# Attention block with layer norm and a gated network on one core: output matmuls over ten steps, max rows by two DMAs in f16, 40 units' lead, and first-pass matmuls in pairs behind the scores

## The reference

```python
qk = (x @ Wqk_w.T + Wqk_b).reshape(b, n, H, E, 2)     # q = qk[..., 0], k = qk[..., 1]
v = (x @ Wv_w.T + Wv_b).reshape(b, n, H, E)
scores = einsum('bhqd,bhkd->bhqk', q, k)
attn = softmax(scores, axis=-1) / sqrt(64)
out = einsum('bhsl,bhlv->bhsv', attn, v) -> (b, n, 64)
x = layernorm(x + out @ Wo_w.T + Wo_b)
# gated network: int4 weights with a float scale for each group of 128 inputs, 1792 inner values
y = einsum('bsi,hi->bsh', silu(x @ Wg.T) * (x @ Wu.T), Wd)
x = layernorm(x + y)
```

## Time and profile before

| | before |
|---|---|
| median of the runs | 572.08 us (571.86, 572.08, 576.48) |
| profiled execution | 576.28 us |
| its span, first to last instruction | 574.5 us |
| mean granted clock of PE | 0.968 |
| PE busy | 531.3 us (92%) |
| DVE busy | 422.3 us (74%) |
| ACT busy | 406.5 us (71%) |
| POOL busy | 234.2 us (41%) |
| chain of waits by engine | PE 72%, DVE 19%, ACT 3%, issue 2%, DMA 2% |
| largest lines of the chain | L842, L854, L871 (network) 50%; L971 (first-pass reduction) 14%; L793 (av) 5%; L726 (first pass) 5%; L760 (output matmul) 3% |
| L971 reductions | 256 of 682 ns mean |
| L557 exponentials | 128 of 1115 ns mean |
| L842, L854, L871 | 448 matmuls each, 379 ns mean (pipelined) |
| L1092, L1112 DVE scaling | 755 and 750 ns mean |

### The profile page before, as it was taken

The page is one execution under the profiler, slowest core; times in us unless marked ns, Lnnn a source line. Parts: engine busy times, 40 slices in busy tenths (PEclk is TensorE's granted clock), DMA queues, the critical chain, the costliest instruction groups (busy, mean ns, idle before and its releaser), DMA issues.

```text
span 574.5 us, 7484 instructions
## 1 busy us (share of the span) xinstructions
PE 531.3 (92%) x2640; PEld 198.7 (35%) x2640; DVE 422.3 (74%) x725; ACT 406.5 (71%) x579; POOL 234.2 (41%) x267
## 2 busy tenths in 40 slices
PE   9897888989889989989999999999999999999992
PEld 3222212222122212214444445444454444544441
DVE  3589796978898799244877678766688667787666
ACT  1430675757677768997788877878878887787881
POOL 8020740002291255263546332673334733338442
PEclk9899597979999999999999999999999999999998
DMA  5593175002231003021004000010000010000101
GB/s 174 160 192 66 40 138 181 1 2 57 91 37 39 3 0 76 2 47 28 1 1 56 18 2 0 2 63 12 0 2 1 0 74 0 2 1 1 73 2 73
DMA packets 29237, 24.59 MB, mean 43 GB/s; under 512 B 19632, under 2 KB 21552, under 8 KB 29200
## 3 DMA queue, kind: packets, MB, share of 16 engines
q1 hardware_dynamic: 25328, 17.56, 11.4%
q0 software_dynamic: 3872, 6.56, 5.9%
HBM read 20.08 MB, written 4.19 MB: 42 GB/s over the span
## 4 chain that ended last, share of the span: by engine, by line
PE 72%; DVE 19%; ACT 3%; issue 2%; DMA 2%; SPq 1%; POOL 0%; POOLq 0%; ACTq 0%; DVEq 0%
PE ps L842 17%; PE ps L854 17%; PE ps L871 16%; DVE mxh L971 14%; PE ps L793 5%; PE ps L726 5%; PE ps L760 3%; PE ps L666 3%; PE ps L778 2%; PE ps L712 2%; ACT pbuf L557 1%; DMA stack<-mp 1%; SPq L335 1%; PE ps L880 1%; DVE st L1010 1%
## 5 line engine op out<-in xcount | busy, mean ns | idle before, releaser
L971 DVE TENSOR_REDUCE mxh<-ps 128x1 f32<-128x512 f32 x256 | 162.1, 682 | 28.4 <-PE ps L726 26.9
L1092 DVE TENSOR_SCALAR ps<-ps,ratio 128x512 f32<-128x512 f32 x168 | 121.8, 755 | 80.9 <-PE ps L854 80.5
L557 ACT ACTIVATE pbuf<-ps,gamma 128x1024 f32<-128x1024 f32 x128 | 135.2, 1115 | 49.7 <-PE ps L778 49.3
L612 ACT ACTIVATE ps<-ps,ratio 128x512 f32<-128x512 f32 x168 | 106.0, 657 | 41.7 <-PE ps L842 41.7
L871 PE MATMUL ps<-stack,wd 128*128 128x512 f16 x448 | 129.5, 379 | 0.6 <-POOL stack L484 0.6
L842 PE MATMUL ps<-arena,wg 128*128 128x512 f16 x448 | 115.3, 379 | 0.1
L854 PE MATMUL ps<-arena,wu 128*128 128x512 f16 x448 | 115.3, 379 | 0.0
L633 ACT ACTIVATE ps<-ps,ratio 128x512 f32<-128x512 f32 x156 | 102.7, 664 | 16.4 <-PE ps L871 16.4
L726 PE MATMUL ps<-stack 64*128 64x512 f16 x256 | 89.6, 407 | 13.6 <-DVE mxh L971 9.3
L482 POOL CAST stack<-pbuf 128x512 f16<-128x512 f32 x56 | 34.1, 609 | 141.3 <-DVE pbuf L1099 141.3
L793 PE MATMUL ps<-pbuf,arena 128*32 128x512 f32 x512 | 71.2, 629 | 0.6 <-ACT pbuf L557 0.6
(11 more groups left out here) (100 smaller groups left out, 330.5 us busy)
## 6 DMA issues: line engine op xcount, KB each, us to landing
arena<-xT SPq DMA_DIRECT2D x16, 256.0 KB, 5.6
x<-x SPq DMA_DIRECT2D x2, 2048.0 KB, 10.1
out<-x SPq DMA_DIRECT2D x3, 1024.0 KB, 4.2
wg<-gq POOLq DMA_DIRECT2D x4, 448.0 KB, 10.3
wu<-uq POOLq DMA_DIRECT2D x4, 448.0 KB, 12.7
wd<-dq POOLq DMA_DIRECT2D x2, 896.0 KB, 10.7
out<-x SPq DMA_DIRECT2D x4, 256.0 KB, 2.4
stack<-mp SPq DMA_DIRECT2D x48, 2.0 KB
```

The costliest lines, as they stand in the source:

```text
L557: nc.scalar.activation(pbuf[:, pi % 4, :].rearrange("p (a n) -> p a n", a=2), ps[:, 2 * (pi % 2):2 * (pi % 2) + 2, :], ACT.Exp, scale=gamm ...
L612: nc.scalar.activation(gbank[t % 2], gbank[t % 2], ACT.Copy, scale=gr[:, t % G, c:c + 1])\
L971: nc.vector.tensor_reduce(mxh[:, f % 2, qh, half:half + 1], ring_bank("first", n, 0), AX.X, ALU.max)\
L1092: nc.vector.tensor_scalar(ubank[t % 2], ubank[t % 2], ur[:, t % G, c:c + 1], None, ALU.mult)\
```

## The change

Eight things change together.

1. PE's order in a step becomes scores, a, b, scores, c, d, (others), av; `ring_at` puts the other uses behind the four units.
2. The output matmuls of a block lie at steps 4, 7, 10, 13 of the next block (ten steps from first to last) instead of 4, 6, 7, 8. The statistics move from steps 9, 10 to 14, 15. DVE's application of block 2's norm (and POOL's splitting) moves from step 12 of the last block into the network's periods 5 to 8, block 3's from periods 7 to 10 into 11 to 14.
3. The maxima are split into three f16 parts before the transpose, on 128x16, inside `combine`; one f16 transpose of 48 columns and one DVE copy (`max_out`) follow. M comes one step later (n+2 divisible by 8) and waits for `s_mrow`.
4. `max_rows` issues two DMAs, each of 24 partitions x 128 f16 into three rows, instead of six.
5. `AHEAD` is 40 instead of 46; the first M stands behind 34 units instead of 37.
6. `place_rows` issues batch 1's rows from two queues: twelve DMAs by POOL, twelve by SP between the scale loads and the second group's max rows.
7. Before step 0 two `put` pieces follow each two units (one piece behind two units once 15 are left), and two puts instead of three precede the first unit.
8. v of batch 1 is transposed into bank 6 and placed by DVE in step 0; `scores(0, 0)` waits only for its own banks, `av(0)` for v.

```diff
-AHEAD = FG + 14
+AHEAD = FG + 8
@@ ring_at
-            f, r = divmod(n + 3, KT)
+            f, r = divmod(n + 2, KT)
...
-            return first[0:2] + other + first[2:4]
-        WO_AT = (4, 6, 7, 8)
+            return first + other
+        WO_AT = (4, 7, 10, 13)
         before = [("first", n, 0) for n in range(AHEAD)]
-        before.insert(FG + 5, ("M", 0, 0))
+        before.insert(FG + 2, ("M", 0, 0))
@@ new, called by SP with jj = 1 and by POOL with jj = 0
+        def place_rows(engine, jj):
+            for kind in range(2):
+                for part in range(2):
+                    for slot in range(4)[half_slots(kind, part)]:
+                        r, at = ROWS * jj + E * slot, kind * HD + jj * HD // 2
+                        src = (high, low)[part][at:at + HD // 2, :]
+                        if kind:
+                            engine.dma_start(ks[1][r:r + E, :, :], src).then_inc(s_stk1[jj], 16)
+                            continue
+                        for k in range(N // TB):
+                            engine.dma_start(qs[1][r:r + E, k, :, :], src[:, k * TB:(k + 1) * TB])\
+                                .then_inc(s_stk1[jj], 16)
@@ max_rows
-                for i in range(3):
-                    for jj in range(2):
-                        r = ROWS * jj + MROW + i
-                        sp.dma_start(qs[b][r:r + 1, k, 2 * g:2 * g + 2, :],
-                                     mp[2 * BT * jj:2 * BT * (jj + 1), f % 2, i, :]).then_inc(s_mld[g], 16)
+                for jj in range(2):
+                    r = ROWS * jj + MROW
+                    sp.dma_start(qs[b][r:r + 3, k, 2 * g:2 * g + 2, :],
+                                 mrows[6 * BT * jj:6 * BT * (jj + 1), f % 2, :]).then_inc(s_mld[g], 16)
@@ SP, between the scale loads and max_rows(1)
+            sp.wait_ge(s_low, 3)
+            sp.wait_ge(s_fill, 6)
+            place_rows(sp, 1)
@@ PE, transpose of v and of the maxima
-                    pe.wait_ge(s_unit, 3 * (b + 1))
+                    if b == 0:
+                        pe.wait_ge(s_unit, 3)
...
-                    pe.wait_ge(s_mxc, u + 1)
-                    mm = nc.tensor.transpose(dst[0:HG * BT, 0:P], mx[:, u % 2, :], ident[:])
+                    pe.wait_ge(s_mrow, u + 1)
+                    mm = nc.tensor.transpose(dst[0:3 * HG * BT, :].bitcast(F16)[:, 0:P], mp[:, u % 2, :], ident16[:])
@@ PE, scores
                 elif pi == 0:
-                    pe.wait_ge(s_vc, 2 * B)
+                    pe.wait_ge(s_projr, 5)
+                else:
+                    pe.wait_ge(s_projr, 6)
+                    pe.wait_ge(s_unit, 6)
@@ PE, main order
-            for n in range(3):
+            for n in range(2):
                 put(n)
...
-                if later and (n < closely or n % 2):
-                    piece(later.pop(0))
+                if n % 2:
+                    for _ in range(2 if len(later) > 15 else 1):
+                        piece(later.pop(0))
+            for p in later:
+                piece(p)
             for n in range(ALL):
                 uses = ring_at(n)
-                late = max(1, len(uses) - (2 if len(uses) >= 4 else 0))
+                early = 2 if uses and uses[0][0] == "first" else 0
                 scores(n, 0)
-                for use in uses[0:1]:
+                for use in uses[0:early]:
                     ring_use(*use)
                 scores(n, 1)
-                for use in uses[1:late + 1]:
+                for use in uses[early:]:
                     ring_use(*use)
                 if n:
                     av(n - 1)
-                for use in uses[late + 1:]:
-                    ring_use(*use)
@@ DVE, combine goes on with the split
+                part = [mp[:, f % 2, :].rearrange("p (j i q) -> p i j q", j=2, i=3)[:, i, :, :] for i in range(3)]
+                nc.vector.tensor_copy(part[0], top).then_inc(s_msp, 1)
+                nc.vector.tensor_tensor(rest, top, part[0], ALU.subtract).then_inc(s_msp, 1)
+                nc.vector.tensor_copy(part[1], rest).then_inc(s_msp, 1)
+                nc.vector.tensor_tensor(part[2], rest, part[1], ALU.subtract).then_inc(s_mrow, 1)
...
-                if n > STEPS and n % STEPS in (9, 10):
+                if n == 0:
+                    place_v(1)
+                if n > STEPS and n % STEPS >= 14:
```

More of the change, by code:

```diff
@@ L37 @@
 MROW = 4 * E
-PARTS = 4 * 2 * (1 + N // TB)
+PARTS = 4 * (1 + N // TB)
 VC = 32
@@ L122, in build @@
         mx = sb("mx", [P, 2, HG * BT], F32)
-        mres = sb("mres", [HG * BT, P], F32)
-        mp = sb("mp", [HG * BT, 2, 3, P], F16)
+        mres = sb("mres", [P, HG * BT], F32)
+        mp = sb("mp", [P, 2, 3 * HG * BT], F16)
+        mrows = sb("mrows", [3 * HG * BT, 2, P], F16)
+        ident16 = sb("ident16", [P, P], F16)
         st = sb("st", [P, BT, 6], F32)
@@ L168, in build @@
         s_kept = sem("rows_kept_in_stack0")
-        s_stk1 = sem("rows_in_stack1")
+        s_stk1 = [sem(f"rows_in_stack1_half{jj}") for jj in range(2)]
         s_rf = sem("ring_full")
@@ L345, in _ @@
             max_rows(3)
-            sp.wait_ge(s_stk1, 16 * PARTS)
+            for jj in range(2):
+                sp.wait_ge(s_stk1[jj], 16 * PARTS)
             sp.wait_ge(s_vt, B)
@@ L424, in _ @@
             pool.wait_ge(s_low, 3)
[L425 to L436, removed]
+            place_rows(pool, 0)
             for g in range(0, G, G // 2):
@@ L473, in _ @@
                     apply(u, s_x1)
-                for t in range(BT):
-                    x1_parts(u, t)
+                    for t in range(BT):
+                        x1_parts(u, t)
             def inner_parts(t):
@@ L491, in _ @@
                     inner_parts(p - 2)
-                if p == 5:
+                if 5 <= p < 5 + BT:
+                    x1_parts(NB - 2, p - 5)
+                if p == 10:
                     inverse(NB - 1)
-                if 7 <= p < 7 + BT:
-                    x1_parts(NB - 1, p - 7)
+                if 11 <= p < 11 + BT:
+                    x1_parts(NB - 1, p - 11)
                 for blk in range(NB - 1):
@@ L678, in vt @@
                     pe.wait_ge(s_projr, 3 * (b + 1))
-                    pe.wait_ge(s_unit, 3 * (b + 1))
+                    if b == 0:
+                        pe.wait_ge(s_unit, 3)
                     for t in range(BT):
-                        mm = nc.tensor.transpose(bank[3][:, t * P:(t + 1) * P], vtmp[:, t * P:(t + 1) * P], ident[:])
+                        mm = nc.tensor.transpose(bank[VTB[b]][:, t * P:(t + 1) * P], vtmp[:, t * P:(t + 1) * P], ident[:])
                     mm.then_inc(s_vt, 1)
@@ L723, in first_pass @@
                 elif n == 2 * H * BT * 2:
-                    pe.wait_ge(s_stk1, 16 * PARTS)
+                    for half1 in s_stk1:
+                        pe.wait_ge(half1, 16 * PARTS)
                 rows = slice(ROWS * jj, ROWS * (jj + 1))
@@ L810, in _ @@
                 piece(p)
-            for n in range(3):
+            for n in range(2):
                 put(n)
-            later = [(put, n) for n in range(3, 6)] + [turn_v] + [(put, n) for n in range(6, len(placed))]
-            closely = len(later)
+            later = [(put, n) for n in range(2, 6)] + [turn_v] + [(put, n) for n in range(6, len(placed))]
             later += projections(1)
@@ L962, in place_v @@
                 for k in range(2):
-                    src = bank[3].rearrange("p (t k h e) -> p t k h e", t=BT, k=2, h=H)[:, :, k, :, :]
+                    src = bank[VTB[b]].rearrange("p (t k h e) -> p t k h e", t=BT, k=2, h=H)[:, :, k, :, :]
                     nc.vector.tensor_copy(vst[b][:, k * BT:(k + 1) * BT, :, 0:E], src).then_inc(s_vc, 1)
@@ L1142, in _ @@
                         attention_stats(NB - 1, 2 * (p - 3) + k)
-                if p == 4:
+                if 5 <= p < 5 + BT:
+                    apply(NB - 2, [p - 5])
+                if p == 9:
                     mean_variance(NB - 1)
-                if 7 <= p < 7 + BT:
-                    apply(NB - 1, [p - 7])
+                if 11 <= p < 11 + BT:
+                    apply(NB - 1, [p - 11])
                 for blk in range(NB - 1):
```

43 lines of the change are left out of this document (20 added, 23 removed).

## The result

The changed kernel takes 586.05 us (median of 4 runs, 584.52 to 589.38) beside 572.14 us for the kernel before on the same chip (571.86 to 576.48): a ratio of 1.0233, interval 1.0166 to 1.0300. It is slower by 2.3%, and by at least 1.7% as the interval goes. The forecast was slower, 579.2 us: the side is right, the time is 6.9 us short, and the median lies on the upper edge of the range (565 to 586). Between the medians the change costs 13.9 us, where the sum had 7.1.

What follows compares the result with a forecast made beforehand. The prediction took the 64 attention steps, a loop through PE and DVE, to bound the kernel. Its terms (11.7 + 2.6 + 0 + 0.4 - 5.5 - 4.9 + 1.9 + 0.9) gave +7.1: 579.2 us median, range 565 to 586.

Steps and rivals of the forecast that it cites:

- the sum: All predicted terms added: +7.1 us, giving 583.4 for a profiled execution and 579.2 for the median.
- Ordinary step, +11.7: Attention steps 1 to 53: one more score slot in the loop lengthens each from 2.49 to 2.71 us, +11.7.
- The end: Last first-pass matmul moves from step 52 to the end of 53, which takes 2.71 instead of 1.84 us: +0.9.
- Rival 1: DVE finds a filled bank at each step's start and keeps the pace: not slower, about 566 us; chance 0.26.
- Other users, +2.6: Output matmuls and transposes behind the four first-pass matmuls cost +0.28 each, +5.0, less savings in waits: +2.6 us.
- max rows, +0.4: Two DMAs instead of six, but a later transpose; no margin at step 8: +0.4 us for two groups.
- Splitting ahead of the transpose, 0: Splitting the maxima on DVE before their transpose takes 1.1 us against 1.07 before: 0.
- The stall of step 8 goes, -5.5: Steps 7 to 9: wd's load issued earlier, so the 3 us stall and the low clock behind it go: -5.5 us.
- rival 3: Wd's load or the 24 pieces delay the max rows and still hold step 8: 583 to 586 us; chance 0.10.
- Start, -4.9: Before the attention steps: earlier projection and scales let step 1 begin at 59.05 instead of 63.97 us: -4.9.
- Low clock at the start, +1.9: First attention steps to 70.4 us: at the 1.2 GHz level the new order loses 4.1, the old 2.2: +1.9 us.
- Rival 2: DVE's starving makes PE wait longer and the clock falls again, two or three more times: 584 to 586 us; chance 0.13.

Runs made afterwards that it cites:

- experiment 2: Kernel before with only PE's new order in a step (scores, a, b, scores, c, d, others, av): 588.96 us, ratio 1.0274.
- experiment 3: Changed kernel with PE's old order in a step, all else as changed (lead 40): 582.73 us, ratio 1.0148 to the kernel before.
- experiment 4: Changed kernel with PE's old order and a lead of 42 units instead of 40: 583.14 us, ratio 1.0187 to the kernel before.
- experiment 7: Changed kernel with PE's old order, lead 42 and wd's load issued behind the second group's max rows: 582.58 us, ratio 1.0191.
- experiment 8: As experiment 7, but GpSimd splits block 0 only after group 5's maxima, and SP turns it behind group 5's max rows: 575.49 us, one run.
- experiment 5: Changed kernel with wd's load issued only when the second group's max rows have landed: 582.96 us, ratio 1.0154 to the kernel before.
- experiment 10: Kernel before with wd's load issued only when the second group's max rows have landed: 569.94 us, ratio 0.9926.
- experiment 11: Kernel before with wd's load late and the change's start, old order, lead 46: 566.07 us, ratio 0.9874.
- experiment 1: Kernel before, unchanged, run again for a second profile: 576.06 us, ratio 1.0011; the profiled execution took 570.72 us.

## Why the prediction was right, and where it was wrong

Step by step, against the first profile of before (576.28 us; the change took 584.52, so +8.2 beside the +7.1 of the sum).

- **Ordinary step, +11.7.** Right: 2.70 for 2.71, with a wait ahead of d and DVE idle for 0.22 ahead of a's reduction (0.3 was forecast). It is 52 x 0.21 = 10.9 and not 53 times: step 53, which had no first-pass matmul before, is counted again in *The end*. Experiments 2 and 3 turn the step length on and off. Rival 1 falls: in the ordinary steps DVE has no bank in hand.
- **Other users, +2.6, and max rows, +0.4.** The single steps are right (4.04 and 3.57 for 4.05 and 3.58), the sum is too high. Steps 19 to 50 grew by 7.7, of which 32 x 0.21 = 6.7 is the first term; with steps 5, 6, 13 to 16 and 52 some 1.9 us remain in all, not 3.0. More was saved than the 0.5 a block I had credited, where output matmuls had stood next to each other and the statistics behind them; no run in the new order separates the two.
- **Splitting ahead of the transpose, 0.** Nearly right in this kernel, for its order: a step with the transpose of the maxima is 3.89, 1.19 beyond an ordinary one, where the pair of steps 5 and 6 before was 1.08 beyond two. The transpose stands behind d, and by then the splitting is done. In the old order it stands ahead of c: PE waits 1.27 for the splitting with a lead of 40, with a lead of 42 the step is 1.55 beyond an ordinary one, and beside GpSimd it is 2.0 to 3.0 longer still (experiments 3, 4, 7 and 8). The working counted DVE's time only and did not name that cover.
- **The stall of step 8 goes, -5.5.** This step failed. Steps 7 to 9 took 14.75 us instead of 13.58; less the ordinary 0.63 that is +0.5. The prediction had the issue time right (67.4 for 66.7), but concluded from it that the load was out of the way, and worked out no end. In the trace of before the load landed 13.9 us after its first issue, which would be 81.3 here, with the rows wanted at 80.7; behind the 24 copies, issued by SP and GpSimd from 60.60 to 69.14, it took 16.9 and landed at 84.26, and the rows issued at 78.10 and 78.89 came with it. This is rival 3's place and price, by its first cause; the 24 pieces are innocent (1.9 us without the load, 1.7 estimated). Experiments 5 and 10 show that the load alone makes the stall in both kernels. Had this step held, the profiled execution would have been 6 us shorter, near 578.5; experiment 5's was 579.38.
- **Start, -4.9.** Nearly right: step 1 at 59.42, so -4.6, and -3.6 against the second profile of before. Experiment 11 has it on its own.
- **Low clock at the start, +1.9, and that nothing else changes with the clock.** Wrong in sign: steps 1 to 4 took 11.95 us after 12.23, steps 17 and 18 10.51 after 11.36. Less the longer ordinary step this is -1.1 and -1.3. I had priced the clock by one execution of before that was low in it for 30.7 us, while another was for 13.7 (experiment 1). For the same reason the 4.2 us between that execution and the median should not have been taken off the sum: the change's own execution lay 1.5 us under its median. Against the second profile of before (570.72) the change's execution is 13.8 us longer, as the medians are, and there the stall is +1.8 (14.75 for 12.32 us, less 0.63) instead of -5.5: these 7.3 us are what the sum lacks (6.7), the other differences nearly cancel.
- **The end, +0.9.** Right for step 53 (2.70 for 1.84). From step 54 on, not in the sum, 0.9 was added; output matmuls and statistics now stand there.

So the sum's agreement on profiled executions (583.4 and 584.5) is partly luck: +6.0 for the stall that stayed, +0.9 from step 54 on and +0.3 for the start, against -4.3 for the clock, -1.1 for the other users and -0.8 for the ordinary step. The loss itself is the first term, which was sized right.

Rival 2, the clock falling again: the changed kernel had 17.1 us at 1.2 GHz, between the two executions of before, and from 121.3 us to the end of the attention steps, in steps of 2.70 to 4.04 with a wait in nearly each, the granted clock stayed at 2.4 GHz. In the changed kernel the rule of the Trainium skill that the prediction quotes, of short idle times that let the clock swing, is not borne out. It is not refuted either: in experiment 11's execution, in the old order, the granted clock fell to 1.2 GHz for 3.4 us from 147.5 us on, and PE's longest wait in the 7.5 us before was this, among others of 0.21 and 0.40:

```profile
145.05 0.39 PE L729 MATMUL ps<-stack 64*128 64x512 f16 x1 [0.80 <-DVE mxh L979]
```

Open: what fixes how often the clock falls from execution to execution. That the row copies slow the load was read from the queue's MB; it was not tried with the copies on one queue. The load has no fixed length to compare with: it took 15.4 us in the second profile of before and 17.1 in experiment 5, where no row copy but SP's load of x (2048 KB) ran beside it, and no run has it alone. So of the stall's two parts (a load that starts beside the copies and ends too late even at 13.9 us, and the 3 us more) only the sum is shown. The lead of 40, the splitting ahead of the transpose and the two DMAs were not put on the kernel before one by one.

## What to carry to other kernels

Where two engines pass banks around in a ring, write the loop down (what lets a bank go, what is queued before the next fill) and count the slots in it: one matmul slot moved into it cost 0.21 us in each of some fifty steps, though PE was waiting in every one of them. A transfer that is moved earlier must be priced among its new neighbours and by its end, not by the time of its issue; a wait that puts it behind the small urgent one cost one line and gained 0.7% (1.3% with the earlier start). When part of a change is undone, look at what the undone part covered.

## What the runs showed of the hardware

- Small DVE operations between SBUF tiles are held up by GpSimd's: 0.17 us became 1.02 to 1.19 us, ending within 0.04 us of GpSimd's operation of 1.15 to 1.26 us (experiments 7 and 8). The Trainium skill (SBUF — State Buffer, section "Who interferes with whom") says that a DVE operation in a 2-port mode, or with two SBUF inputs beside a GpSimd operation that reads SBUF, shares an exclusive pair of ports, and the later one is blocked fully. The traces agree for the subtraction with its two inputs (1.19). The cast (1.05) has one input; that it ran in such a mode no view here shows.
- The last of two DMAs of 6 KB each, issued during a load of 2 x 896 KB from memory, landed 5.6 us after its issue, 0.2 behind the load, instead of 1.9 (experiment 5: 1.94). In the trace of before the last of six of 2 KB landed 4.9 us after its issue (83.12 to 88.05), 2.3 ahead of the load: held up, but not to its end.
- The kernel before, unchanged, took 570.7 to 576.3 us in two profiled executions, by 17 us more of the 1.2 GHz level.
